# A graph-attention kernel on one core: the first turned block's copy, the order of SP's transfers, and row 5's high parts

## The chip, the cores and the metric

The kernel runs on one core of one Trainium2 chip. The time is the device time of one execution in microseconds, and the number compared is the median of several executions. The engines of the core are TensorE (PE in the profile), VectorE (DVE), ScalarE (ACT), GpSimd (POOL) and the sync engine (SP). Each works through its own instructions in order and waits on semaphores where another engine or a DMA has to be ready first. In this kernel nearly all DMAs are issued by SP.

## What is computed

```
Wh   = x @ W0.T                                # x: 4096 x 256
sim  = Wh @ Wh.T / (|Wh_i| |Wh_j| + 1e-8)
mask = (adj > 0) | eye                         # adj: 4096 x 4096
x1   = layernorm(x + softmax(where(mask, sim, -inf)) @ Wh)

m    = (adj > 0)
agg  = m @ x1 / max(rowsum(m), 1)
comb = [x1 @ W_self + b_self, agg @ W_nb + b_nb] @ W_comb + b_comb
out  = layernorm(x1 + relu(comb))
```

The similarity is symmetric, so the exponential of a block of scores serves twice: for the target rows it was made for, and turned (transposed) for the other side. The mask is not symmetric, so each of the two uses has its own block of `adj`.

## The kernel before

The 4096 nodes are 32 blocks of 128, in G = 8 groups of four blocks. The work is a triangle of group pairs, taken row by row: row `a` has its diagonal step (a, a) and then the pairs (a, b) with b > a. Row 0 uses an older scheme that the change does not touch. Rows 1 to 6 use the scheme called "far", with 6 + 5 + 4 + 3 + 2 + 1 = 21 pairs. Row 7 has only a diagonal. Behind the triangle come the value products and the second layer, which are almost only TensorE work.

One far pair (a, b) has eight tiles. Four are direct: TensorE multiplies the exponentials of blocks b*4 + r with the adjacency as columns of row a. In this text they are D0 to D3 (`attend_direct`). Four are turned: the same exponentials, transposed by DMA, give group b's partial sums. They are B0 to B3 (`attend_block`), one block of group b each. Every tile is 12 matmuls. TensorE's order within a pair is D0, D1, D2, D3, then S0' B0, S1' B1, S2' B2, S3' B3, where S0' to S3' are the next pair's scores (six matmuls each). In the last pair of a row (b = 7) the scores between are those of the next row's diagonal: none ahead of B0, one set ahead of each of B1, B2 and B3. The one ahead of B3 also waits until VectorE has masked the first diagonal tile (`prob_ready`).

The blocks B0 to B3 accumulate in two PSUM slots, `turned_ps(x % 2)`. So B2 writes where B0 was, and it waits (`turned_copied`, in `attend_block`) until VectorE has added B0's result into group b's partial sums in `big`. That addition is `block_copied` (L1079); for blocks 0 to 3 of the pair this text calls it C0 to C3. B3 waits for C1 in the same way, and the next pair's B0 and B1 for C2 and C3.

VectorE does for each pair, all in `pair_far`:

- K0 to K3 (`keep`, L1086): turns an adjacency unit of 128 x 1024 int32 into a float16 mask. It waits for the unit's load, `adj_loaded`.
- L0 to L3 (`low`, L1119): the low parts of the exponentials. Each waits for ScalarE's high part (L729), which follows ScalarE's exponential (L678), which follows the scores.
- M0 to M3 (`masked_parts`, L1091 and L1092): mask times high and mask times low, for the direct tiles.
- X0 to X3 (the same lines): the same for the turned tiles. X0 and X1 wait for part 0 of the transposes, X2 and X3 for part 1 (`far_loaded`).
- pieces of the previous row's residual and normalisation (`norm_work`), one list per row, handed out by `beside` and, for the first three, by the diagonal step.

Its order in a pair is K0 L0 C0 M0, L1 C1 M1, K1 L2 C2 M2, L3 C3 M3, K2 K3, X0 X1 X2 X3, where the C's belong to the pair before. So C0 of a pair stands behind X3, and behind the next pair's K0 and L0. In the last pair of a row C0 stands behind X3, the remaining pieces and `attention_out` (L1004), at the start of the next row's diagonal.

SP's order for a pair is in its own `pair_far`: wait for K0, load unit 0 of the next pair, wait for L1, issue the two transposes of part 0 (`turn_far`, L489), store unit 0's mask; wait for K1, load unit 1, store mask 1, wait for L3, issue the two transposes of part 1; load and store units 2 and 3. A load is 512 KB, a mask store 128 KB.

ScalarE makes exponentials, high parts and the byte masks (`unit_kept`, L713). The high half of a row's normalised features, `x1_hi`, is made by VectorE for rows 0 to 5 (`split_x1`, L1034) and by ScalarE for rows 6 and 7 (`x1_head`).

## Time and profile before

| | |
|---|---|
| median of 3 runs | 867.37 us (867.26 to 870.83) |
| the profiled execution, whole | 864.09 us |
| its span, first to last instruction | 862.3 us |
| mean granted TensorE clock | 0.996 |
| PE busy | 836.2 us, 97% |
| DVE busy | 589.6 us, 68% |
| ACT busy | 354.6 us, 41% |
| DMA, mean over the span | 172 GB/s; in the far rows 220 to 250 GB/s |

The far rows run from about 189 us to 580 us, row 7's diagonal ends at 590 us, and from there to the end TensorE computes with no wait but in the last few microseconds. Busy shares are means over the whole span; what bounds a stage has to be read from the waits in it. VectorE's recorded durations overlap a little (0.42 us recorded where the next instruction starts 0.34 us later), so a sum of durations is an upper bound of the time they take.

### The profile page before, as it was taken

What the parts mean: (1) busy time and instruction counts of PE and PEld (TensorE: products, weight loads), DVE (VectorE), ACT (ScalarE), POOL (GpSimd) and SP (SyncE); (2) the same over time, 40 slices, a digit from 0 to 9 for tenths busy, and PEclk for the clock granted to TensorE, in tenths of its full rate; (3) what the DMA queues carried; (4) which work ended last, traced back from release to release, by engine and by line L of the source; (5) the groups of instructions that cost most, each with busy time, mean ns of one, the idle gap of its engine ahead of it and who ended that gap; (6) DMA issues with size and microseconds to landing.
All of it is one profiled execution on the core that took longest, in us unless ns stands there. A gap on an engine that the chain in (4) does not pass through costs nothing.

```text
span 862.3 us, 18015 instructions
## 1 busy us (share of the span) xinstructions
PE 836.2 (97%) x6703; PEld 668.7 (78%) x6703; DVE 589.6 (68%) x1420; ACT 354.6 (41%) x577; POOL 74.0 (9%) x177
## 2 busy tenths in 40 slices
PE   8999999999999999999999999989999999999997
PEld 6867777777767677777777677768888888888886
DVE  2777887888688787888887989888445333333333
ACT  4867666665555555646546546445110000000000
POOL 2400000000000000000001101111101011100111
PEclk9999999999999999999999999999999999999999
DMA  8955666479999899999999999985303312330300
GB/s 211 242 153 171 163 175 174 126 203 225 229 220 232 241 225 233 236 253 226 239 259 223 233 246 230 247 181 220 51 8 128 117 51 85 111 114 22 116 20 19
DMA packets 202862, 147.93 MB, mean 172 GB/s; under 512 B 137505, under 2 KB 169778, under 8 KB 201746
## 3 DMA queue, kind: packets, MB, share of 16 engines
q1 hardware_dynamic: 202578, 146.33, 65.4%
q8 instruction: 53, 0.87, 0.4%
q0 software_dynamic: 192, 0.41, 0.2%
q14 instruction: 39, 0.32, 0.2%
HBM read 95.83 MB, written 20.99 MB: 135 GB/s over the span
## 4 chain that ended last, share of the span: by engine, by line
issue 80%; PE 10%; POOL 6%; DVE 2%; ACT 1%; POOLq 1%; DMA 0%; DVEq 0%; SPq 0%; ACTq 0%
POOL rstd L619 4%; PE ps L1294 4%; POOL var_eps L617 2%; PE ps L1384 1%; PE ps L1386 1%; PE ps L1385 1%; PE ps L1324 1%; PE ps L1326 1%; PE ps L1325 1%; ACT mask L690 1%; PE ps L1378 1%; DMA feat<-xT 0%; ACT prob_hi L685 0%; DVE feat L829 0%; DVE work L974 0%
## 5 line engine op out<-in xcount | busy, mean ns | idle before, releaser
L1384 PE MATMUL ps<-feat,prob_hi 128*128 128x257 f16 x1024 | 280.7, 274 | 14.5 <-DVE big L1079 12.5
L1386 PE MATMUL ps<-feat,prob_lo 128*128 128x257 f16 x1024 | 279.9, 273 | 0.0
L1385 PE MATMUL ps<-feat,prob_hi 128*128 128x256 f16 x1024 | 278.9, 272 | 0.0
L1554 PE MATMUL ps<-big,mgroup 128*128 128x257 f16 x992 | 219.2, 273 | 0.0
L1555 PE MATMUL ps<-big,mgroup 128*128 128x256 f16 x992 | 219.2, 273 | 0.0
L1384 PEld LDWEIGHTS ps<-feat,prob_hi 128*128 128x128 f16 x1024 | 99.9, 98 | 43.8 <-issue 18.7
L678 ACT ACTIVATE work<-ps 128x512 f32<-128x512 f32 (+2 forms) x144 | 79.9, 557 | 119.1 <-PE ps L1326 115.5
L1385 PEld LDWEIGHTS ps<-feat,prob_hi 128*128 128x128 f16 x1024 | 100.6, 98 | 24.4
L713 ACT ACTIVATE mask<-work 128x1024 fp8e4<-128x1024 f16 x84 | 86.2, 1050 | 76.6 <-DVE work L1086 76.6
L1386 PEld LDWEIGHTS ps<-feat,prob_lo 128*128 128x128 f16 x1024 | 99.7, 97 | 13.7
L1554 PEld LDWEIGHTS ps<-big,mgroup 128*128 128x128 fp8e4 x992 | 97.1, 98 | 12.1
L1555 PEld LDWEIGHTS ps<-big,mgroup 128*128 128x128 fp8e4 x992 | 97.1, 98 | 11.2
L1324 PE MATMUL ps<-unitT_lo,unitT_hi 128*128 128x512 f16 (+3 forms) x288 | 103.9, 362 | 1.0 <-DVE work L974 0.8
L1325 PE MATMUL ps<-unitT_hi 128*128 128x512 f16 (+3 forms) x288 | 103.8, 362 | 0.0
L1326 PE MATMUL ps<-unitT_hi,unitT_lo 128*128 128x512 f16 (+3 forms) x288 | 103.8, 362 | 0.0
L1091 DVE TENSOR_TENSOR prob_hi<-work,mgroup 128x512 f16<-128x512 f16 x168 | 70.5, 419 | 41.3 <-DMA mgroup<-mgroup 38.1
L981 DVE SCALAR_TENSOR_TENSOR prob_lo<-work,prob_hi 128x512 f16<-128x512 f32 x88 | 60.4, 687 | 22.6 <-ACT prob_hi L685 20.9
L1246 DVE TENSOR_SCALAR deg<-ps,ones,mix_scales 128x1 f32<-128x1 f32 x32 | 8.8, 275 | 94.7 <-PE ps L1555 94.7
L617 POOL TENSOR_TENSOR var_eps<-meanvar,ln_eps 128x1 f32<-128x1 f32 x64 | 16.6, 259 | 662.4 <-DVE meanvar L1021 441.5
L1092 DVE TENSOR_TENSOR prob_lo<-work,mgroup 128x512 f16<-128x512 f16 x168 | 70.1, 417 | 0.0
L1119 DVE SCALAR_TENSOR_TENSOR mgroup<-work,mgroup 128x512 f16<-128x512 f32 x84 | 57.7, 687 | 16.3 <-ACT mgroup L729 16.0
L685 ACT ACTIVATE prob_hi<-work 128x512 f16<-128x512 f32 x88 | 53.5, 625 | 33.9 <-DVE work L964 13.1
(130 smaller groups left out, 959.1 us busy)
## 6 DMA issues: line engine op xcount, KB each, us to landing
adj_sb<-adjT SPq DMA_DIRECT2D x128, 512.0 KB, 4.6
mask_spill<-mask SPq DMA_DIRECT2D x128, 128.0 KB, 4.1
mgroup<-mask_spill SPq DMA_DIRECT2D x8, 2048.0 KB, 8.3
xres<-x SPq DMA_DIRECT2D x8, 512.0 KB, 5.4
out<-rows SPq DMA_DIRECT2D x32, 128.0 KB, 1.7
feat<-xT SPq DMA_DIRECT2D x7, 512.0 KB, 7.1
norm_bc<-norm_row_dram SPq DMA_DIRECT2D x7, 256.0 KB, 4.1
mgroup<-mgroup SPq DMA_TRANSPOSE x84, 4.1
```

The costliest lines, as they stand in the source:

```text
L678: act.activation(expo[:, r, first:], score_ps(r)[:, first:], ACT.Exp, scale=1.0 / (UNIT_SCALE * UNIT_SCALE)).then_inc(exp_ready, 1)
L713: act.activation(mask[:, u % 4, :], kept(m), ACT.Copy, saturate=False).then_inc(mask_ready, 1)
L1091: dve.tensor_tensor(shaped(prob_hi[:, s, :]), adj, high, ALU.mult).then_inc(prob_ready, 1)
L1092: dve.tensor_tensor(shaped(prob_lo[:, s, :]), adj, low, ALU.mult).then_inc(prob_lo_ready, 1)
L1324: pe.matmul(to, unitT_hi[:, jb, k], unitT_lo[:, tgt, k], start=(k == 0), stop=False)
L1325: pe.matmul(to, unitT_hi[:, jb, k], unitT_hi[:, tgt, k], start=False, stop=False)
L1326: ins = pe.matmul(to, unitT_lo[:, jb, k], unitT_hi[:, tgt, k], start=False, stop=(k == KD - 1))
L1384: pe.matmul(acc(D + 1), prob_hi[:, s, cols], feat_hi_of(g)[:, r, 0:D + 1], start=start, stop=False)
L1385: pe.matmul(acc(D), prob_hi[:, s, cols], feat_lo_of(g)[:, r, :], start=False, stop=False)
L1386: return pe.matmul(acc(D + 1), prob_lo[:, s, cols], feat_hi_of(g)[:, r, 0:D + 1], start=False, stop=stop)
L1554: pe.matmul(agg_ps(q, D + 1), lhsT, z_hi_of(g)[:, r, 0:D + 1], start=(jb == 0), stop=False)
L1555: ins = pe.matmul(agg_ps(q, D), lhsT, z_lo_of(g)[:, r, :], start=False, stop=(jb == NB - 1))
```

## The change

Three things move, and nothing is computed otherwise.

1. VectorE makes C0 inside the turned part of its own pair: behind X1 and ahead of X2. Where the row goes on, the next pair's K0 and L0 go there too, ahead of C0.
2. SP issues the part-0 transposes ahead of load 0, and the part-1 transposes ahead of load 1.
3. ScalarE makes `x1_hi` of row 5. VectorE's four L1034 of that row are gone, and its low parts come one block later in the list of pieces.

```diff
+ACT_X1 = G - 3
@@ SP, pair_far
                 for m in range(4):
                     slot = (u0 + m) % 4
+                    if m < 2:
+                        turn_far(a, b, m)
                     sync.wait_ge(kept_ready, 4 * k + m + 1)
...
-                    if m == 0:
-                        turn_far(a, b, 0)
...
-                    if m == 1:
-                        turn_far(a, b, 1)
@@ ScalarE, pair_far
+                early_x1 = a - 1 == ACT_X1
+                if early_x1:
+                    x1_head(a - 1, 0)
                 unit_kept(u0 + 2, 2, 4 * k + 3)
+                if early_x1:
+                    x1_head(a - 1, 1)
                 unit_kept(u0 + 3, 3, 4 * k + 4)
+                if early_x1:
+                    x1_head(a - 1, 2)
+                    x1_head(a - 1, 3)
@@ VectorE, split_x1 and norm_work
-                if a < G - 2:
+                if a < ACT_X1:
...
-                lag = 1 if a < G - 2 else 2
+                lag = 1 if a < ACT_X1 else 2
@@ VectorE, diagonal
-                        block_copied(G - 1, j, t0 - GB + j)
-                        if j == 0:
+                        if j:
+                            block_copied(G - 1, j, t0 - GB + j)
+                        else:
                             dve.wait_ge(prob_lo_ready, t0)
@@ VectorE, pair_far
                 for r in range(GB):
+                    if r == 2:
+                        keep_unit(a, b, 1)
+                    if r or n == 0:
+                        if r == 0:
+                            keep_unit(a, b, 0)
+                        low_part(a, b, r)
+                        if n:
+                            block_copied(b - 1, r, t0 - GB + r)
...
                 for x in range(GB):
+                    if x == 2:
+                        if b < G - 1:
+                            keep_unit(a, b + 1, 0)
+                            low_part(a, b + 1, 0)
+                        block_copied(b, 0, t0 + GB)
```

VectorE between pair (2, 6) and pair (2, 7), before: X2 and X3 (the first four rows), a piece of normalisation, then the next pair's K0, L0, the copy C0 and M0. The "..." stands for the branch around a correction that is never taken here.

```order
L1091 TENSOR_TENSOR prob_hi<-work,mgroup 128x512
L1092 TENSOR_TENSOR prob_lo<-work,mgroup 128x512
L1091 TENSOR_TENSOR prob_hi<-work,mgroup 128x512
L1092 TENSOR_TENSOR prob_lo<-work,mgroup 128x512
L1028 TENSOR_SCALAR feat<-summed,meanvar,rstd 128x256
L1086 TENSOR_SCALAR work<-adj_sb 128x1024
...
L1119 SCALAR_TENSOR_TENSOR mgroup<-work,mgroup 128x512
L1079 TENSOR_TENSOR big<-big,ps 128x257
L1091 TENSOR_TENSOR prob_hi<-work,mgroup 128x512
L1092 TENSOR_TENSOR prob_lo<-work,mgroup 128x512
```

The same place in the changed kernel, from the end of X1 on (lines have shifted: L1094 is K, L1118 is L, L1087 is C, L1099 and L1100 are M and X, L1035 is the piece).

```order
L1094 TENSOR_SCALAR work<-adj_sb 128x1024
...
L1118 SCALAR_TENSOR_TENSOR mgroup<-work,mgroup 128x512
L1087 TENSOR_TENSOR big<-big,ps 128x257
L1099 TENSOR_TENSOR prob_hi<-work,mgroup 128x512
L1100 TENSOR_TENSOR prob_lo<-work,mgroup 128x512
L1099 TENSOR_TENSOR prob_hi<-work,mgroup 128x512
L1100 TENSOR_TENSOR prob_lo<-work,mgroup 128x512
L1035 TENSOR_SCALAR feat<-summed,meanvar,rstd 128x256
L1099 TENSOR_TENSOR prob_hi<-work,mgroup 128x512
L1100 TENSOR_TENSOR prob_lo<-work,mgroup 128x512
```

K0, L0 and C0 have moved from behind X3 and the piece to ahead of X2; M0 now follows the piece directly.

SP in one pair of row 2, before: load 0, part 0, store 0, load 1, store 1, part 1, load 2.

```order
L389 DMA adj_sb<-adjT 128x2x512
L489 DMA_TRANSPOSE mgroup<-mgroup 128x8x128 x2
L412 DMA mask_spill<-mask 128x1024
L389 DMA adj_sb<-adjT 128x2x512
L412 DMA mask_spill<-mask 128x1024
L489 DMA_TRANSPOSE mgroup<-mgroup 128x8x128 x2
L389 DMA adj_sb<-adjT 128x2x512
```

The same pair in the changed kernel.

```order
L490 DMA_TRANSPOSE mgroup<-mgroup 128x8x128 x2
L390 DMA adj_sb<-adjT 128x2x512
L413 DMA mask_spill<-mask 128x1024
L490 DMA_TRANSPOSE mgroup<-mgroup 128x8x128 x2
L390 DMA adj_sb<-adjT 128x2x512
L413 DMA mask_spill<-mask 128x1024
L390 DMA adj_sb<-adjT 128x2x512
```

Load 0 moved behind part 0, and load 1 with store 1 behind part 1.

ScalarE at the end of pair (6, 7) in the changed kernel, from the last high part (L733) to the next diagonal's first exponential (L677); before, the four rows L711 (`x1_head` of row 5) are not there and the masks L717 (L713 before) follow each other.

```order
L733 ACTIVATE mgroup<-work 128x512
L711 ACTIVATE big<-feat 128x256
L717 ACTIVATE mask<-work 128x1024
L711 ACTIVATE big<-feat 128x256
L717 ACTIVATE mask<-work 128x1024
L711 ACTIVATE big<-feat 128x256 x2
L669 COMPARE_AND_BRANCH
L669 UNCONDITIONAL_BRANCH
L677 ACTIVATE work<-ps 128x512
```

The last two of the four stand directly ahead of that exponential.

## Rows read from the trace of the kernel before

**Rows 1.** Waits view, PE: who it waited for, us in total, times, longest.

```profile
PE ps L1384 <- DVE big L1079: 12.5, 11, 2.5
PE ps L1384 <- DVE prob_lo L1092: 1.0, 1, 1.0
```

**Rows 2.** Timeline, PE: start us, us, instruction, idle before and releaser.

```profile
206.27 0.27 PE L1384 MATMUL ps<-feat,prob_hi 128*128 128x257 f16 x1 [1.60 <-DVE big L1079]
...
287.11 0.27 PE L1384 MATMUL ps<-feat,prob_hi 128*128 128x257 f16 x1 [1.41 <-DVE big L1079]
...
376.95 0.27 PE L1384 MATMUL ps<-feat,prob_hi 128*128 128x257 f16 x1 [1.19 <-DVE big L1079]
...
508.01 0.27 PE L1384 MATMUL ps<-feat,prob_hi 128*128 128x257 f16 x1 [1.70 <-DVE big L1079]
...
550.36 0.27 PE L1384 MATMUL ps<-feat,prob_hi 128*128 128x257 f16 x1 [1.50 <-DVE big L1079]
...
571.54 0.28 PE L1384 MATMUL ps<-feat,prob_hi 128*128 128x257 f16 x1 [1.01 <-DVE prob_lo L1092]
...
579.13 0.35 PE L1384 MATMUL ps<-feat,prob_hi 128*128 128x257 f16 x1 [2.50 <-DVE big L1079]
```

**Rows 3.** Windows: PE, PEld, DVE, ACT, POOL busy (count), PEclk, DMA share, GB/s.

```profile
400.00:450.00 50.00, 50.00 (x386) 37.45 (x385) 44.28 (x113) 26.52 (x37) 1.83 (x4) 1.00 0.97 252
576.70:579.10 2.40, 0.00 (x0) 0.00 (x1) 2.37 (x8) 0.46 (x1) 0.00 (x0) 1.00 0.23 45
579.13:582.65 3.52, 3.52 (x17) 2.56 (x18) 1.82 (x5) 0.63 (x1) 0.00 (x0) 0.52 1.09 214
```

**Rows 4.** Timeline, DVE, pair (2, 6): X2, then K0, L0 and C0.

```profile
357.51 0.42 DVE L1091 TENSOR_TENSOR prob_hi<-work,mgroup 128x512 f16<-128x512 f16 x1 [2.09 <-DMA mgroup<-mgroup]
...
359.52 0.69 DVE L1086 TENSOR_SCALAR work<-adj_sb 128x1024 f16<-128x1024 int32 x1
360.13 0.68 DVE L1119 SCALAR_TENSOR_TENSOR mgroup<-work,mgroup 128x512 f16<-128x512 f32 x1
360.73 0.41 DVE L1079 TENSOR_TENSOR big<-big,ps 128x257 f32<-128x257 f32 x1
```

**Rows 5.** Timeline, PE, the same pair: the first matmul of B0 and of B2.

```profile
356.24 0.27 PE L1384 MATMUL ps<-feat,prob_hi 128*128 128x257 f16 x1
...
361.48 0.27 PE L1384 MATMUL ps<-feat,prob_hi 128*128 128x257 f16 x1
```

**Rows 6.** Timeline, ACT, the same pair: the exponential and high part behind S0'.

```profile
356.44 0.60 ACT L678 ACTIVATE work<-ps 128x512 f32<-128x512 f32 x1 [1.36 <-PE ps L1326]
357.07 0.63 ACT L729 ACTIVATE mgroup<-work 128x512 f16<-128x512 f32 x1
```

**Rows 7.** Timeline, SP's issues, the same pair: load 0, part 0, load 1, part 1.

```profile
344.68 0.37 SPq L389 DMA_DIRECT2D adj_sb<-adjT  x1
346.93 2.60 SPq L489 DMA_TRANSPOSE mgroup<-mgroup  x2
...
350.20 1.17 SPq L389 DMA_DIRECT2D adj_sb<-adjT  x1
...
351.98 3.51 SPq L489 DMA_TRANSPOSE mgroup<-mgroup  x2
```

**Rows 8.** Waits view, DVE: its waits for the transposes.

```profile
DVE prob_hi L1091 <- DMA mgroup<-mgroup: 38.1, 19, 3.5
```

**Rows 9.** Source view of L389, the adjacency loads.

```profile
DMA to landing us min/median/max: 3.7/4.6/9.1
```

**Rows 10.** Source view of L489, the transposes.

```profile
DMA to landing us min/median/max: 3.1/4.1/6.3
```

**Rows 11.** Timeline, DVE, end of row 4: X2, C0, the next diagonal's first mask.

```profile
504.11 0.43 DVE L1091 TENSOR_TENSOR prob_hi<-work,mgroup 128x512 f16<-128x512 f16 x1 [2.15 <-DMA mgroup<-mgroup]
...
507.45 0.42 DVE L1079 TENSOR_TENSOR big<-big,ps 128x257 f32<-128x257 f32 x1
507.78 0.69 DVE L960 SCALAR_TENSOR_TENSOR work<-adj_sb,work 128x512 f32<-128x512 int32 x1
```

**Rows 12.** Lines view by form, DVE: the high parts of rows 0 to 5.

```profile
L1034 DVE TENSOR_SCALAR big<-feat 128x256 f16<-128x256 f32 x24 | 6.9, 286 | 0.1
```

More of the change, by code:

```diff
@@ L707, in diagonal, with x1_head @@
                         unit_mask(u % 4, j - 1, 16 * (u // 4))
+            def x1_head(a, q):
+                act.wait_ge(rows_ready, a * GB + q + 1)
+                act.activation(x1_hi_of(a)[:, q, :], x1_of(a)[:, q, :], ACT.Copy, scale=NORM_SCALE).then_inc(x1_hi_ready, 1)
             def unit_kept(u, m, count):
@@ L788, in value_heads @@
                                    ACT.Copy, scale=VALUE_SCALE).then_inc(z_hi_ready, 1)
-            def x1_head(a, q):
-                act.wait_ge(rows_ready, a * GB + q + 1)
-                act.activation(x1_hi_of(a)[:, q, :], x1_of(a)[:, q, :], ACT.Copy, scale=NORM_SCALE).then_inc(x1_hi_ready, 1)
             for q in range(2):
@@ L1032, in split_x1 @@
                 dve.wait_ge(rows_ready, a * GB + q + 1)
-                if a < G - 2:
+                if a < ACT_X1:
                     chain.join(chain.step(dve.tensor_scalar(x1_hi_of(a)[:, q, :], x1_of(a)[:, q, :], NORM_SCALE, None, ALU.mult)))
                 else:
-                    dve.wait_ge(x1_hi_ready, (a - G + 2) * GB + q + 1)
+                    dve.wait_ge(x1_hi_ready, (a - ACT_X1) * GB + q + 1)
                 dve.scalar_tensor_tensor(out=x1_lo_of(a)[:, q, :], in0=x1_of(a)[:, q, :], scalar=NORM_SCALE,
@@ L1092, in masked_parts, with keep_unit, low_part @@
                 dve.tensor_tensor(shaped(prob_lo[:, s, :]), adj, low, ALU.mult).then_inc(prob_lo_ready, 1)
+            def keep_unit(a, b, m):
+                n = b - a - 1
+                t0, _, u0 = (first + more for first, more in zip(tiles_before(a), (GB + n * STEP_TILES, 0, 2 + n * 4)))
+                if n:
+                    keep(u0 + m, m, t0 - STEP_TILES + 2 * (m + 1) if m < 2 else t0, u0 + m - 3)
+                else:
+                    keep(u0 + m, m, t0, u0 - 1 + m // 2)
+            def low_part(a, b, r):
+                n = b - a - 1
+                t0, f0, _ = (first + more for first, more in zip(tiles_before(a), (GB + n * STEP_TILES, GB + n * GB, 0)))
+                damping(a, b * GB + r, scores_before(a) + GB + n * GB + r, f0 + r, r)
+                dve.wait_ge(far_hi_ready, GB * (far_before(a) + n) + r + 1)
+                dve.wait_ge(prob_lo_ready, t0 - STEP_TILES + r + 1 if n else t0)
+                dve.scalar_tensor_tensor(out=far_parts[:, 1, r, :], in0=expo[:, r, :], scalar=PROB_SCALE, in1=far_parts[:, 0, r, :],
+                                         op0=ALU.mult, op1=ALU.subtract).then_inc(far_lo_ready, 1)
             def pair_far(a, b, between):
                 n = b - a - 1
-                t0, f0, u0 = (first + more for first, more in zip(tiles_before(a), (GB + n * STEP_TILES, GB + n * GB, 2 + n * 4)))
-                c0 = scores_before(a) + GB + n * GB
+                t0 = tiles_before(a)[0] + GB + n * STEP_TILES
                 k = far_before(a) + n
@@ L1106, in beside @@
                             between.pop(0)()
-                def keep_unit(m):
-                    if n:
-                        keep(u0 + m, m, t0 - STEP_TILES + 2 * (m + 1) if m < 2 else t0, u0 + m - 3)
-                    else:
-                        keep(u0 + m, m, t0, u0 - 1 + m // 2)
-                def low(r):
-                    dve.wait_ge(far_hi_ready, GB * k + r + 1)
-                    dve.wait_ge(prob_lo_ready, t0 - STEP_TILES + r + 1 if n else t0)
-                    dve.scalar_tensor_tensor(out=far_parts[:, 1, r, :], in0=expo[:, r, :], scalar=PROB_SCALE, in1=far_parts[:, 0, r, :],
-                                             op0=ALU.mult, op1=ALU.subtract).then_inc(far_lo_ready, 1)
-                for r in range(GB):
-                    if r % 2 == 0:
-                        keep_unit(r // 2)
-                    damping(a, b * GB + r, c0 + r, f0 + r, r)
-                    low(r)
-                    if n:
-                        block_copied(b - 1, r, t0 - GB + r)
+                for r in range(GB):
+                    if r == 2:
[4 more added lines that the diff above has]
+                        low_part(a, b, r)
+                        if n:
+                            block_copied(b - 1, r, t0 - GB + r)
                     dve.wait_ge(kept_ready, 4 * k + r // 2 + 1)
@@ L1132, in pair_far @@
                     beside()
-                keep_unit(2)
-                keep_unit(3)
+                keep_unit(a, b, 2)
+                keep_unit(a, b, 3)
                 beside()
```

## The prediction

> **What bounds the kernel now.** Four views, in this order. The page gives PE 97% busy, so the end is set by PE's work and the little idle time in it. The waits view for PE says what that idle time is: 12.5 us in 11 waits for VectorE's L1079, and 1.0 us in one wait for a turned tile [rows 1]. The timeline says where. L1079 is the copy of a finished block, and each of the 11 waits stands at the first matmul of a B2, whose PSUM slot B0 still holds. Four are at row ends, those of rows 1, 2, 4 and 5 (1.41, 1.19, 1.70 and 1.50, together 5.80 us). One is at the end of row 6 (2.50 us). Six are in the middle of rows: 1.60 us in the first pair of row 1, and five more that hold what is left, 12.5 - 5.80 - 2.50 - 1.60 = 2.6 us [rows 1, 2].
>
> The windows show something the waits view does not price. After the 2.50 us wait the granted clock is 0.52 for the next 3.52 us, that is the 1.2 GHz level, against 1.00 before and elsewhere [rows 3]. At half speed 3.5 us of work should have taken half as long, so this stretch lost about 1.7 us. No wait of 1.7 us or less is followed by it.
>
> VectorE is not the bound, but it is the engine that is late. In pair (2, 6) it waits 2.09 us at X2 for the part-1 transposes, and C0 comes behind X3, a piece, K0 and L0 [rows 4]. There B2 starts at 361.48, right behind its predecessor, and C0 ended at 361.14, with 0.3 us to spare [rows 4, 5]. That is how near every pair is to a wait. In all, VectorE waits 38.1 us for transposes, in 19 of the 21 pairs [rows 8].
>
> **Part 1: C0, with K0 and L0, ahead of X2.** No instruction is added. What matters is whether the new place adds a wait. I place the changed order in pair (2, 6). From B0 to B2 PE takes 5.24 us for four equal groups, 1.31 each, so B0 ends near 357.55 [rows 5]. C0 needs that, and L0 stands ahead of it. L0 needs ScalarE's high part, which ends at 357.70, since S0' ended only near 356.4 [rows 6]. L0 takes 0.60 us, so 358.3; C0 0.4, so 358.7; X2 is two instructions of 0.34, so 359.4. B2 wants both C0 and X2 by 361.4. So the new wait of VectorE (behind it are X2 and X3, and for X2 PE waits) takes the place of the wait for the transposes and leaves 2 us, where there were 0.3. The five small mid-row waits and the one of 1.60 should all go: **-4.2 us**. What comes next is C1 for B3. It follows X3, the piece, M0 and L1: 359.4 + 0.7 + 0.4 + 0.7 + 0.6, plus its own 0.4, gives 362.2, and B3 starts 2.6 us behind B2, at 364.1. Not late.
>
> At a row's end C0 stands alone ahead of X2, and there B0 is long finished when VectorE waits for the transposes, so C0 fits into that wait (2.15 us in row 4). What was behind it is then earlier by only 0.33 us. The next thing late is the first mask of the next diagonal: the scores ahead of B3 wait for it. In row 4 it ended near 508.4, so it would end near 508.1, while B2, starting 1.70 us earlier at 506.3 and 1.3 long, would end at 507.6 [rows 2, 11]. So about 0.5 us of row 4's 1.70 stays if X2 comes no sooner. The same working leaves 0.4 in row 5, 0.2 in row 1 and nothing in row 2, 1.1 together; earlier transposes (part 2) should return half of it. I take 0.6 kept of 5.80: **-5.2 us**.
>
> **Row 6.** Here VectorE has one pair for all the pieces and has no wait at X2, so C0's move alone shifts nothing behind it. B2 could start near 576.6 instead of 579.13 [rows 2]. The first mask ended near 579.5; with part 3 it ends near 578.4, against B2's end at 577.7. So about 0.8 of the 2.50 us stays: -1.7. A wait of 0.8 us is shorter than the many in this trace behind which the clock stays at 1.00 [rows 2], so the 1.7 us of half clock go as well. The 1.01 us wait for X0 [rows 2] shrinks by one high part less ahead of it, 0.29 us. Row 6 in all: 1.7 + 1.7 + 0.3 = **-3.7 us**.
>
> **Part 2: transposes ahead of loads.** No DMA is added. Part 0 moves past load 0, which waits for an early K0, so it gains little. Part 1 moves past load 1 and store 1. In pair (2, 6) it was issued 0.1 us behind store 1, and its first waits end at L3, so its issue gains 0.5 us at most; load 1, 512 KB issued 1.8 us ahead of it [rows 7], is no longer in its way. X2's data is then ahead of need. I book nothing for this beyond the 0.5 us at the row ends above.
>
> The price is on the loads. Load 0 was issued at 344.68 and would now be issued behind part 0, at 349.5 [rows 7], while K0 is wanted 4 us earlier than before. For K0 to hide it has to start at 357.1 (0.6 ahead of the high part's end), which gives the load 7.5 us; for B2 not to wait, at 359.2, which gives 9.6 us. Loads landed 3.7 to 9.1 us from issue, median 4.6 [rows 9]. Lower end 0, since the median is well inside; upper end 15 pairs (those with a next pair in their row) times the excess over 9.6. I take 0, nearest the median. Load 1 is issued near 355 instead of 350.2, and K1 comes near 363: covered.
>
> At this place the skill speaks against the change. The Trainium skill, "DMA: Bandwidth & Descriptors", section "Queues, rings and completion order", says that each DMA engine takes one queue's descriptors in ring order, so a load issued behind the transposes is read behind them. By that, and from rows: the second transpose is issued 1.3 us ahead of load 0 and lands after 4.1 (at most 6.3) [rows 7, 10], and then 4.6 us of load follow, so 7.4 us typically and 9.6 at worst, which just fits both limits. The sum stays as it is; the margin is thin, and this is the rival that ends slower.
>
> **Part 3: row 5's high parts on ScalarE.** Four instructions of 0.286 us leave VectorE [rows 12], 1.14 us, already booked in row 6. ScalarE gains four, and the last two stand ahead of the next diagonal's first exponential and wait for VectorE's pieces behind X1 and X2. That exponential would then end near 576.2, ahead of the mask that needs it (start 577.8). Cost 0; if VectorE's pieces came 2 us later it would cost that excess.
>
> **The sum.** 4.2 + 5.2 + 3.7 = 13.1 us. The profiled execution is 864.09 us whole, so it would be 851.0; the median of before is 867.37, 3.3 above it, and I apply the saving to the median: **854.3 us**. Behind 590 us PE has no wait until its last tile, and the pieces and transposes it needs there shift with row 7's end, so nothing is given back.
>
> **Rivals.**
> - *Row 6 keeps its wait and the half clock.* Its VectorE is the busiest (2.37 of 2.40 us ahead of the wait [rows 3]). If the new exponentials' order or the pieces hold the first mask, 1.7 + 1.7 us stay: 857.7. Chance 0.12.
> - *The wait moves on to the next late thing, C1 or the diagonal's first mask,* and half the gain is lost: 861. The slack found for C1 speaks against it, the row ends for it. Chance 0.11.
> - *DMA is the bound.* Its share is 0.97 [rows 3] and pairs follow each other no faster than their transfers: 867, or L0 ahead of C0 waits so long for ScalarE that C0 is no earlier, the change not doing what it says: also 867. But over 400 to 450 PE has no idle time at 252 GB/s, so the transfers can keep up. Chance 0.07 for both.
> - *Load 0 late: slower.* K0 stands ahead of X2 now, so a late load stops PE in 15 pairs. It decides from 9.6 us landing time on, breaks even at 9.6 + 13.1/15 = 10.5, and at 11.1 us costs 15 x 1.5 = 22.5: 867.4 - 13.1 + 22.5 = 876.8. The longest landing, 9.1 us, speaks against it. Chance 0.05.
> - *Everything goes,* the row ends' 0.6, row 6's 0.8 and the rest of X0's wait with it, 0.7: 852.2. Chance 0.05.
>
> **How the numbers follow.** The forecast of 854.3 has the chance left, 0.60. What a measurement of this kernel can tell from no change is about 0.5%, 4.3 us. Faster by more than that, below 863.0: 0.60 + 0.12 + 0.11 + 0.05 = 0.88. Within it: 0.07. Slower: 0.05. The range is from 851.3 (the best case and 0.9 for the spread of runs) to 861.5 (the third case); it leaves out 0.12, and some of the cases' own spread.
>
> **What the changed profile would show.** PE's waits for the copy line gone in mid-row, and at most 0.5 us in some row ends, now for the mask ahead of the diagonal scores. VectorE's 38 us wait for transposes mostly replaced by waits for ScalarE's high part at L0 and for PE at C0. The granted clock at 1.00 through the end of row 6. No wait of K for an adjacency load over 2 us. If VectorE waits on loads in most pairs and PE behind it, the fourth case holds and I am wrong; if PE's waits are gone and the time is still above 863, what I took as PE's own work was not.

## The result and the profile of the changed kernel

The changed kernel takes 855.62 us (median of 4, 855.06 to 857.24) against 867.54 us of the kernel before on the same chip (median of 4, 867.26 to 870.83). The ratio is 0.9857, with an interval of 0.983 to 0.9885. The forecast was 854.3, the range 851.3 to 861.5. So the sign and the size of the median are right. The profile shows that two steps under it were not.

The profiled execution of the changed kernel took 857.24 us whole (span 855.4), against 864.09 before. That is 6.9 us, where the sum said 13.1. First the waits of PE, as in [rows 1]: us in total, times, longest.

```profile
PE ps L1343 <- DVE work L971: 4.8, 4, 1.5
...
PE ps L1403 <- DVE prob_lo L1100: 2.2, 3, 1.6
...
PE ps L1343 <- DVE work L967: 0.5, 1, 0.5
```

The waits for the block copy, 12.5 us in [rows 1], are gone to the last one. What stands in their place is a wait of the scores (L1343) for VectorE's masks of the next diagonal (L971, and in row 6 L967), and a larger wait for X0 (L1100). L967 is the whole mask of a diagonal's first tile, and L967 and L971 together are the mask of a later one. The timeline of PE says where (start us, us, instruction, idle before and releaser); it is the counterpart of [rows 2].

```profile
289.50 0.39 PE L1343 MATMUL ps<-unitT_lo,unitT_hi 128*128 128x512 f16 x1 [1.24 <-DVE work L971]
...
451.22 0.39 PE L1343 MATMUL ps<-unitT_lo,unitT_hi 128*128 128x512 f16 x1 [1.19 <-DVE work L971]
...
508.73 0.39 PE L1343 MATMUL ps<-unitT_lo,unitT_hi 128*128 128x512 f16 x1 [0.87 <-DVE work L971]
...
539.34 0.28 PE L1403 MATMUL ps<-feat,prob_hi 128*128 128x257 f16 x1 [0.28 <-DVE prob_lo L1100]
...
551.70 0.39 PE L1343 MATMUL ps<-unitT_lo,unitT_hi 128*128 128x512 f16 x1 [1.51 <-DVE work L971]
...
565.29 0.28 PE L1403 MATMUL ps<-feat,prob_hi 128*128 128x257 f16 x1 [0.33 <-DVE prob_lo L1100]
568.36 0.28 PE L1403 MATMUL ps<-feat,prob_hi 128*128 128x257 f16 x1 [1.57 <-DVE prob_lo L1100]
...
575.35 0.28 PE L1343 MATMUL ps<-unitT_lo,unitT_hi 128*128 128x256 f16 x1 [0.47 <-DVE work L967]
```

No copy wait is left in mid-row. At the ends of rows 1, 3, 4 and 5 there are 1.24 + 1.19 + 0.87 + 1.51 = 4.81 us, where the row ends of before had 5.80 and row 3 had none. These four are not the wait for the diagonal's first mask that the prediction named. The waiting scores are 128x512, those of the next row's first pair, behind B3, and what they wait for is the mask of the diagonal's third tile. Only in row 6 do the scores ahead of B3 (128x256) wait for the first mask, 0.47 us. X0's wait there is 1.57, with 0.33 just ahead of it, and 0.28 is new in row 5.

VectorE's waits say what replaced the 38.1 us for transposes [rows 8].

```profile
DVE mgroup L1118 <- ACT mgroup L733: 36.1, 38, 2.5
...
DVE summed L1022 <- DMA xres<-x: 10.9, 6, 2.5
DVE big L1087 <- PE ps L1405: 5.8, 4, 1.8
...
DVE prob_hi L1099 <- DMA mgroup<-mgroup: 0.6, 1, 0.6
```

The low parts now wait for ScalarE's high parts, and the last copies for PE, as was foreseen. The line between them was not foreseen: 10.9 us of waiting for `xres`, the residual's rows of `x`, where before there was one wait of 0.7. L1022 is the first piece of the residual; it stands in the next row's diagonal behind the masks of the first two tiles, and the third tile's mask (L967 and L971) follows it. The five waits in rows 1 to 5 are 2.38, 1.27, 2.33, 1.83 and 2.48 us, and PE waits behind each but the 1.27 of row 2. In row 4, timelines of the changed kernel's SP and DVE:

```profile
500.70 0.43 SPq L548 DMA_DIRECT2D xres<-x  x1
```

```profile
507.19 0.48 DVE L1022 SCALAR_TENSOR_TENSOR summed<-summed,rsum_s,xres 128x256 f32<-128x256 f32 x1 [1.83 <-DMA xres<-x]
507.59 0.42 DVE L1087 TENSOR_TENSOR big<-big,ps 128x257 f32<-128x257 f32 x1
507.93 0.42 DVE L967 SCALAR_TENSOR_TENSOR work<-adj_sb,work 128x256 f32<-128x256 int32 x1
508.26 0.42 DVE L971 SCALAR_TENSOR_TENSOR work<-adj_sb,ps 128x256 f32<-128x256 int32 x1
```

And in the same row of the kernel before, where nothing waits:

```profile
504.32 0.48 SPq L549 DMA_DIRECT2D xres<-x  x1
```

```profile
510.52 0.48 DVE L1015 SCALAR_TENSOR_TENSOR summed<-summed,rsum_s,xres 128x256 f32<-128x256 f32 x1
```

VectorE wants the residual at 507.19 - 1.83 = 505.36 instead of 510.52, so 5.2 us sooner, and the load is issued only 3.6 us sooner. It also lands later after its issue. The source view gives us from issue to landing (minimum, median, maximum) of the kernel's eight loads of this kind; first before, then changed.

```profile
DMA to landing us min/median/max: 3.7/5.4/6.1
```

```profile
DMA to landing us min/median/max: 3.9/6.6/8.2
```

The middle of a row is as it was placed on paper. Pair (2, 6) in the changed kernel, DVE: L0, C0 and X2, the counterpart of [rows 4].

```profile
353.93 0.69 DVE L1118 SCALAR_TENSOR_TENSOR mgroup<-work,mgroup 128x512 f16<-128x512 f32 x1 [2.53 <-ACT mgroup L733]
354.53 0.42 DVE L1087 TENSOR_TENSOR big<-big,ps 128x257 f32<-128x257 f32 x1
354.87 0.42 DVE L1099 TENSOR_TENSOR prob_hi<-work,mgroup 128x512 f16<-128x512 f16 x1
```

B2 starts in that pair at 357.67 without a wait, 2.7 us behind C0's end, where before there were 0.3 us between them.

Last, the windows around row 6's wait (us, PE, PEld, DVE, ACT, POOL busy and count, granted clock, DMA share, GB/s), against [rows 3].

```profile
573.00:575.30 2.30, 1.87 (x16) 1.36 (x14) 2.30 (x8) 0.49 (x1) 0.00 (x0) 1.00 0.53 138
575.35:578.00 2.65, 2.65 (x27) 2.42 (x28) 2.45 (x7) 2.39 (x4) 0.00 (x0) 1.00 1.16 226
```

The clock stays at its 2.4 GHz level, where it had fallen to 0.52.

**The account.** From PE's last wait in row 0 to the first value product, before took 168.13 to 590.45, 422.3 us; changed, it takes 168.99 to 583.59, 414.6 us. "The stage" below is this stretch. It is 7.7 us shorter; the 0.86 us by which it starts later is ahead of anything the change touches and makes 6.9 of it. The terms that the rows of these two executions give: mid-row -4.2; row ends 4.81 against 5.80, -1.0; row 6's mask 0.47 against 2.50, -2.0; its half clock -1.7; X0 and its like 1.57 + 0.33 + 0.28 against 1.01, +1.2. The sum is -7.7.

### The profile page after: what moved, and what is told of

The parts are those of the page before. It is cut to its first block, busy times and chain, and to the rows that moved or that the text cites. A ratio compares the mean times of both kernels' runs of the same rounds, so it can differ in the third digit from the quotient of the medians.

```text
span 855.4 us, 18019 instructions
## 1 busy us (share of the span) xinstructions
PE 835.1 (98%) x6703; PEld 668.4 (78%) x6703; DVE 587.6 (69%) x1416; ACT 354.9 (41%) x581; POOL 71.6 (8%) x177
## 4 chain that ended last, share of the span: by engine, by line
issue 80%; PE 8%; POOL 6%; DVE 2%; ACT 2%; DMA 1%; POOLq 1%; SPq 0%; DVEq 0%; ACTq 0%
POOL rstd L618 4%; PE ps L1313 2%; POOL var_eps L616 2%; PE ps L1403 1%; PE ps L1405 1%; PE ps L1404 1%; DMA unitT_lo<-feat 1%; PE ps L1343 1%; PE ps L1345 1%; PE ps L1344 1%; PE ps L1397 1%; ACT mask L689 0%; SPq L434 0%; ACT rows L631 0%; ACT feat L643 0%
## 5 line engine op out<-in xcount | busy, mean ns | idle before, releaser
L677 ACT ACTIVATE work<-ps 128x512 f32<-128x512 f32 (+2 forms) x144 | 79.7, 555 | 109.0 <-PE ps L1345 105.5
L717 ACT ACTIVATE mask<-work 128x1024 fp8e4<-128x1024 f16 x84 | 86.2, 1049 | 68.4 <-DVE work L1094 68.4
L1343 PE MATMUL ps<-unitT_lo,unitT_hi 128*128 128x512 f16 (+3 forms) x288 | 103.7, 362 | 6.4 <-DVE work L971 4.8
L1405 PEld LDWEIGHTS ps<-feat,prob_lo 128*128 128x128 f16 x1024 | 99.5, 97 | 13.5
L1118 DVE SCALAR_TENSOR_TENSOR mgroup<-work,mgroup 128x512 f16<-128x512 f32 x84 | 57.9, 689 | 36.2 <-ACT mgroup L733 36.1
L1099 DVE TENSOR_TENSOR prob_hi<-work,mgroup 128x512 f16<-128x512 f16 x168 | 70.6, 420 | 3.4 <-DMA mgroup<-mgroup 0.6
L1100 DVE TENSOR_TENSOR prob_lo<-work,mgroup 128x512 f16<-128x512 f16 x168 | 70.3, 419 | 0.0
```

Source lines behind the costliest of these rows:

```text
L677: act.activation(expo[:, r, first:], score_ps(r)[:, first:], ACT.Exp, scale=1.0 / (UNIT_SCALE * UNIT_SCALE)).then_inc(exp_ready, 1)
L717: act.activation(mask[:, u % 4, :], kept(m), ACT.Copy, saturate=False).then_inc(mask_ready, 1)
L1099: dve.tensor_tensor(shaped(prob_hi[:, s, :]), adj, high, ALU.mult).then_inc(prob_ready, 1)
L1100: dve.tensor_tensor(shaped(prob_lo[:, s, :]), adj, low, ALU.mult).then_inc(prob_lo_ready, 1)
L1343: pe.matmul(to, unitT_hi[:, jb, k], unitT_lo[:, tgt, k], start=(k == 0), stop=False)
L1405: return pe.matmul(acc(D + 1), prob_lo[:, s, cols], feat_hi_of(g)[:, r, 0:D + 1], start=False, stop=stop)
```

## The experiments

Every experiment's ratio is to runs of the kernel before made with it, in one of three batches. Their medians are 865.99 us for the three parts apart, 867.40 for the changed kernel once more, the changed kernel without part 2, the residual loaded early and C0 alone, and 865.25 for K0 and L0 alone, both runs on row 6, and the early residual without part 2. The ratios are estimates from all the runs and differ a little from the quotient of the medians.

### The three parts apart

Part 1 alone: SP's order and row 5's high parts stay as they were before. Against the changed kernel:

```diff
-ACT_X1 = G - 3
+ACT_X1 = G - 2
@@ SP, pair_far
-                    if m < 2:
-                        turn_far(a, b, m)
...
+                    if m == 0:
+                        turn_far(a, b, 0)
...
+                    if m == 1:
+                        turn_far(a, b, 1)
```

> Only part 1 of the change: VectorE makes K0, L0 and C0 ahead of X2; SP's order and row 5's high parts are as before. Theory A (the place of C0 makes PE's waits, the transposes only fill VectorE's idle time): PE's 12.5 us of waits for the copy line go but for a rest at row ends, the time is 10 to 12 us below before, and VectorE still waits for the transposes at X2, some 10 to 20 us in all in place of 38. Theory B (the late part-1 transposes make C0 late, and the SP order is what counts): PE's waits move from the copy line to X2's lines, and the time is at most 5 us below before.

It takes 852.52 us, ratio 0.9847 (0.981 to 0.9885), with a stage of 411.7 us: part 1 alone is at least as fast as the whole change. The waits of PE and of DVE:

```profile
PE ps L1405 <- DVE prob_lo L1102: 2.4, 3, 1.8
PE ps L1345 <- DVE work L969: 2.1, 2, 1.6
```

```profile
DVE summed L1024 <- DMA xres<-x: 2.9, 3, 1.2
DVE prob_hi L1101 <- DMA mgroup<-mgroup: 2.7, 3, 1.3
```

The copy's line is gone and the row ends are clear but for 0.57 us in row 4, for the first mask, and 0.19 in row 5, for the third (the other 1.56 us are row 6's). VectorE waits 2.9 us for the residual, not 10.9. And it waits only 2.7 us for the transposes, in the old order of SP: most of the 38 us were time in which it had nothing else to do.

Part 2 alone: only SP's order, which is the first piece of the change's diff.

> Only part 2: SP issues the transposes ahead of loads 0 and 1; everything else is as before. Theory A: VectorE's wait at X2 shrinks from 38 us to 20 or less, C0 comes up to 1 us earlier, and since the five small mid-row waits are 0.3 to 0.7 us each and the four at row ends 1.2 to 1.7, some 4 to 6 us are gained; row 6 keeps its 2.5 us and its half clock. Theory B: nearly all of the change's 12 us are gained. Theory C (the loads pay for it): VectorE waits for adjacency loads at K and the time is above before.

859.31 us, 0.9925 (0.9901 to 0.9949), stage 417.9. DVE's waits:

```profile
DVE prob_hi L1089 <- DMA mgroup<-mgroup: 26.8, 17, 2.9
...
DVE summed L1013 <- DMA xres<-x: 9.0, 6, 2.3
```

By itself part 2 gains, since X2 is on the way to C0 there and VectorE waits 11 us less in sum for its transposes. The price is already in the second line: 9.0 us for the residual, and behind it 1.5 us of PE's waits for the third mask, in rows 1, 2 and 4.

Part 3 alone: only row 5's high parts, the change's pieces on ScalarE and in `split_x1` and `norm_work`.

> Only part 3: ScalarE makes row 5's high parts, as in the changed kernel. Expected by my working: row 6 alone moves, by 0.3 us at X0 and 0.9 to 1.1 us at C0, so 1.2 to 1.4 us, and up to 3 us if the wait that is left, 1.4 us, no longer brings the half clock behind it. Rival: ScalarE's waits for VectorE's pieces hold the next diagonal's first exponential, and the time is that of before or 1 us above.

862.69 us, 0.9961 (0.993 to 0.9993). The profiled execution's row 6, PE (X0, then B2):

```profile
574.21 0.28 PE L1393 MATMUL ps<-feat,prob_hi 128*128 128x257 f16 x1 [0.78 <-DVE prob_lo L1101]
...
580.79 0.27 PE L1393 MATMUL ps<-feat,prob_hi 128*128 128x257 f16 x1 [1.49 <-DVE big L1088]
```

Against [rows 2] the wait for X0 falls from 1.01 to 0.78 and B2's from 2.50 to 1.49, so 1.2 us, about the 1.14 that four instructions took from VectorE. The median is 3.3 us below that of the runs beside it, more than these two waits, but the interval reaches from 0.6 to 6 us; what the rest is was not shown.

The kernel before, once more:

> The kernel before, unchanged, for a second profile. Its first profiled execution took 864.09 us where its median was 867.4. If its waits vary from execution to execution (the transposes' landing times decide them), this profile shows more than 13.5 us of PE waits for VectorE in the far rows, some 16 to 17 us where it takes 867; if they do not vary, the 3.3 us lie elsewhere, in the first 60 us or the tail.

861.05 us in this one execution, stage 418.7 against 422.3 of the first profile. The copy's waits are 10.3 us in 10 instead of 12.5 in 11; at the row ends they are 3.46 instead of 5.80, in mid-row 4.33 and 4.21. And the clock stays at 1.00 behind row 6's wait: from its end to the first value product it is 9.66 us here and 11.32 in the first profile, for the same work. The two together, 2.2 and 1.7 us, are about the difference of 3.6. Executions of before differ by this much, which matters for the account below.

### Which part costs: the changed kernel without part 2, and a residual loaded early

The changed kernel, once more, in one batch with the next two and with C0 alone:

> The changed kernel once more, on the same chip as the three below, so that they can be compared with it. Theory A (from the first runs: part 2 holds back the residual's load at row ends, and gives nothing that part 1 has not given): ratio 0.985 to 0.987, VectorE waits about 11 us for the residual's load in 6 waits, and PE about 5 us in 4 or 5 waits for a diagonal's mask. Rival B (the 10.9 us of that wait were one execution's luck): this profile shows them at 3 us or less.

855.29 us, 0.9875 (0.9847 to 0.9904), with 10.0 us for the residual. The third mask's waits at the row ends come to 3.82 us, in all five rows. Set beside the 3.46 to 5.80 us of the two profiles of before, the row ends gained little or nothing by the change.

Parts 1 and 3, with SP's order of before (the diff of part 1 alone, with `ACT_X1 = G - 3` kept):

> Parts 1 and 3 without part 2: SP keeps the old order. Theory A: 2 to 4 us faster than the changed kernel, since the residual's load is issued and lands earlier; VectorE waits 3 us or less for it; 1 us or so faster than part 1 alone by row 6. Rival C (part 2 pays by its earlier transposes): equal to the changed kernel or slower, with VectorE waiting over 10 us for transposes.

850.76 us, 0.9828 (0.9799 to 0.9856), stage 409.2. This is 4.5 us less than the changed kernel beside it. DVE waits 2.0 us for the residual and 3.3 us for the transposes. So part 2 costs about 4.5 us once part 1 is there, and its own object, the transposes' wait, is worth 3 us of an engine that is not the bound. What part 2 did bring is the little that the prediction booked for it: without it PE waits in row 4 for the diagonal's first mask, where the prediction worked out 0.5 us, and with it this wait is nowhere.

```profile
500.37 0.28 PE L1345 MATMUL ps<-unitT_lo,unitT_hi 128*128 128x256 f16 x1 [0.60 <-DVE work L969]
```

The changed kernel, with the residual's load of rows 1 to 5 moved in SP's queue: in the row's last pair, right behind the part-1 transposes and so ahead of loads 1 to 3, instead of behind all of them.

```diff
@@ SP, pair_far
                     if m < 2:
                         turn_far(a, b, m)
+                    if m == 1 and b == G - 1 and a < G - 2:
+                        sync.wait_ge(summed_ready, a * GB)
+                        sync.dma_start(xres[:, :, :], x_v[a]).then_inc(xres_loaded, 16)
@@ SP, behind the row's pairs
-                wait(sync, summed_ready, a * GB)
-                sync.dma_start(xres[:, :, :], x_v[a]).then_inc(xres_loaded, 16)
+                if not FIRST_FAR <= a < G - 2:
+                    wait(sync, summed_ready, a * GB)
+                    sync.dma_start(xres[:, :, :], x_v[a]).then_inc(xres_loaded, 16)
```

> The changed kernel, with one more move: in the last pair of rows 1 to 5 SP issues the residual's load right behind the part-1 transposes, ahead of load 1, not behind the last store. Theory A: the waits for the residual's load go (from 11 us to 1 or less, row 0's), the waits of PE for a diagonal's mask shrink from 5 us to 1 or less, and the time is 3 to 4 us below the changed kernel. Rival D (PE's waits at row ends come from the diagonal's own chain, mirror and exponential): the VectorE waits go, PE's stay, and the time is that of the changed kernel within 1 us.

849.49 us, 0.9811 (0.9783 to 0.9839), stage 408.0: the fastest, 5.8 us under the changed kernel beside it. The waits of DVE and, from PE's timeline, all that is left of waits for VectorE between 200 and 600 us:

```profile
DVE summed L1026 <- DMA xres<-x: 0.9, 1, 0.9
```

```profile
533.37 0.28 PE L1407 MATMUL ps<-feat,prob_hi 128*128 128x257 f16 x1 [0.25 <-DVE prob_lo L1104]
...
559.81 0.28 PE L1407 MATMUL ps<-feat,prob_hi 128*128 128x257 f16 x1 [1.19 <-DVE prob_lo L1104]
...
566.80 0.28 PE L1347 MATMUL ps<-unitT_lo,unitT_hi 128*128 128x256 f16 x1 [0.47 <-DVE work L971]
```

The masks' waits at the ends of rows 1, 3, 4 and 5 are all gone with the residual's. That the residual's load held PE through the third tile's mask is thus shown, not only read from the order.

The same without part 2 (parts 1 and 3, SP's old order; the residual's load again right behind the part-1 transposes, which there is behind load 1 and store 1):

> Parts 1 and 3 with the old order of SP, but the residual's load of rows 1 to 5 issued behind the part-1 transposes of the row's last pair. Theory A (part 2 gives nothing once part 1 is there): as fast as the changed kernel with the early residual's load, 0.980 to 0.982 of before, within 1 us of it. Rival: 1 to 2 us slower than that one, with VectorE waiting 3 us or more for transposes.

851.08 us, 0.9847 (0.9818 to 0.9876), stage 409.2. In this batch the kernel with all three parts, the early residual and a small change in row 6 (the last experiment below, which gains nothing by that change) takes 849.58. So with the residual out of its way part 2 is worth about 1.5 us, where with it in the way it cost 4.5. In the profiled executions the stages are 409.2 and 408.4 us and PE's waits in them 2.1 and 2.0; where the 1.5 us come from stays open.

### What part 1 consists of

Part 1 moves two things, C0 and the next pair's K0 and L0. C0 alone (K0 and L0 stay at the pair's start), against part 1 alone:

```diff
@@ VectorE, pair_far
-                    if r or n == 0:
-                        if r == 0:
-                            keep_unit(a, b, 0)
-                        low_part(a, b, r)
-                        if n:
-                            block_copied(b - 1, r, t0 - GB + r)
+                    if r == 0:
+                        keep_unit(a, b, 0)
+                    low_part(a, b, r)
+                    if n and r:
+                        block_copied(b - 1, r, t0 - GB + r)
...
                     if x == 2:
-                        if b < G - 1:
-                            keep_unit(a, b + 1, 0)
-                            low_part(a, b + 1, 0)
                         block_copied(b, 0, t0 + GB)
```

> Of the change only the copy C0 moved ahead of X2; K0 and L0 stay behind X3, and SP and row 5's high parts are as before. Theory A (PE waited for C0 and for nothing else): as fast as part 1 as a whole, 0.984 to 0.987 of before. Rival E (K0 and L0 have to use VectorE's idle time, or C1 and M0 become late by their 1.2 us): PE waits for M0 or for C1 in mid-row, some 0.5 us in a third of the 15 pairs, and the time is 2 to 3 us above part 1 alone.

864.60 us, 0.9981 (0.9961 to 1.0001), stage 423.3: hardly anything. PE's waits and DVE's wait for PE:

```profile
PE ps L1401 <- DVE prob_lo L1102: 5.3, 7, 1.8
PE ps L1341 <- DVE work L969: 4.4, 5, 1.7
...
PE ps L1401 <- DVE big L1089: 2.9, 7, 1.2
```

```profile
DVE big L1089 <- PE ps L1403: 24.6, 19, 2.4
```

C0 now stands where B0 is not finished yet, and VectorE waits 24.6 us for PE with nothing else ahead. X2 and X3 then come late, and so do K0 and L0 behind them, and PE waits mostly for masked turned tiles and the diagonal's first mask instead of for the copy. The theory that the copy's new place is what counts falls.

K0 and L0 alone, with C0 where it was, behind X3:

```diff
@@ VectorE, pair_far, against the kernel before
                 for r in range(GB):
-                    if r % 2 == 0:
-                        keep_unit(r // 2)
...
-                    low(r)
+                    if r == 2:
+                        keep_unit(a, b, 1)
+                    if r or n == 0:
+                        if r == 0:
+                            keep_unit(a, b, 0)
+                        low_part(a, b, r)
...
                 for x in range(GB):
+                    if x == 2 and b < G - 1:
+                        keep_unit(a, b + 1, 0)
+                        low_part(a, b + 1, 0)
```

> The other half of part 1: K0 and L0 ahead of X2, C0 stays behind X3 and the pieces (at row ends where it was). SP and row 5's high parts as before. Theory F (VectorE has no time to wait for PE at C0 unless the next pair's K0 and L0 are out of the way; what counts is that 1.2 us of work go into its idle time): C0 comes 0.5 to 1.2 us earlier than before, the six mid-row waits go (4.2 us in the first profile), the five at row ends and row 6 stay, and the time is 4 to 7 us below before. Theory G (only C0 ahead of X2 helps, together with K0 and L0): no mid-row wait goes, and the time is that of before within 2 us.

858.10 us, 0.9924 (0.9896 to 0.9951), stage 416.5. PE, first mid-row wait and row 4's end:

```profile
203.97 0.27 PE L1402 MATMUL ps<-feat,prob_hi 128*128 128x257 f16 x1 [0.15 <-DVE big L1088]
...
501.74 0.27 PE L1402 MATMUL ps<-feat,prob_hi 128*128 128x257 f16 x1 [1.58 <-DVE big L1088]
```

The six mid-row waits have shrunk to this one of 0.15 us, though the copy has not passed X2 and X3: 1.3 us of work had left the stretch ahead of it and filled the idle time behind X1, and VectorE's wait for transposes fell from 38 to 10.0 us. The row ends (4.1 us in all, 1.58 of it in row 4, where it was 1.70) and row 6's 2.50 stay, since there is no next pair's K0 and L0 there. So in the middle of rows it is the work moved into the idle time that pays, and C0's own move pays at row ends, where X2's wait is the idle time: about 7 us for the first alone, 2 us (within its uncertainty) for the second alone, 13.5 us for both.

### Row 6

The kernel before, with C0 moved in row 6 only:

```diff
@@ VectorE, diagonal
-                        block_copied(G - 1, j, t0 - GB + j)
+                        if j or a < G - 1:
+                            block_copied(G - 1, j, t0 - GB + j)
@@ VectorE, pair_far
                 for x in range(GB):
+                    if x == 2 and a == G - 2:
+                        block_copied(b, 0, t0 + GB)
```

> The kernel before, with the copy C0 ahead of X2 in row 6's single pair alone. Of PE's waits only the longest, 2.50 us, changes: by my working 1.1 us of it stay. Theory H (a long wait lowers PE's clock only in some executions, and the clock is a large part of how executions of one kernel differ): 1.5 to 3.5 us below before in the median, the mean granted clock of its executions 0.001 or so above before's. Rival: no clock effect, 1.2 to 1.5 us below and the same mean clock.

864.40 us, 0.9999 (0.9971 to 1.0026). PE waits 1.57 us for the first mask where it waited 2.50 for the copy:

```profile
578.43 0.28 PE L1327 MATMUL ps<-unitT_lo,unitT_hi 128*128 128x256 f16 x1 [1.57 <-DVE work L960]
```

The wait falls by 0.9 us, as the trace has it, and the median by 0.85 us, which is within the uncertainty. The 2 to 3 us that a half clock gone as well would have brought are not seen, though the interval, which reaches to 2.5 us, does not quite exclude them.

Row 6 is VectorE's. In the version with the early residual the pieces of normalisation in row 6 were put off, so that X0 comes sooner (places by which so many pieces are done):

```diff
+ROW6_PIECES = (0, 1, 2, 3, 4, 5, 7, 9, 12, 14)
@@ VectorE, pair_far, beside
-                    for _ in range(place * share // (STEP_TILES + 1) - (place - 1) * share // (STEP_TILES + 1)):
+                    done = ROW6_PIECES if a == G - 2 else [p * share // (STEP_TILES + 1) for p in range(STEP_TILES + 2)]
+                    for _ in range(done[place] - done[place - 1]):
```

> The changed kernel with the early residual's load, and in row 6 two of the pieces of normalisation handed out behind X0 and not ahead of it. Theory J (in row 6 VectorE's own chain sets X0, so what PE gained before comes to a wait there): PE's wait of 1.2 us at X0 goes to 0.3 or less; the pieces come later, so the wait for the diagonal's first mask, 0.5 us, grows by 0 to 0.5; 0.5 to 1.2 us faster than without. Rival K (row 6 as a whole is VectorE-bound, the work only moves): the wait at X0 goes, the one for the mask grows by as much, and the time is equal within 0.4 us.

849.58 us, 0.9829 (0.98 to 0.9858), stage 408.4: no gain. PE in row 6:

```profile
559.93 0.28 PE L1409 MATMUL ps<-feat,prob_hi 128*128 128x257 f16 x1 [0.68 <-DVE prob_lo L1105]
...
567.56 0.28 PE L1349 MATMUL ps<-unitT_lo,unitT_hi 128*128 128x256 f16 x1 [1.11 <-DVE work L972]
```

1.19 + 0.47 has become 0.68 + 1.11. VectorE's work in row 6 sets the end of the row, and this order only moves the place where PE waits for it.

## Why the prediction came out as it did

**What bounds the kernel.** Right. PE's idle time in the far rows was the whole of what could be had, and with nearly all of it gone the stage is at 408 us.

**Part 1, mid-row, -4.2.** Right in size and in its working: the wait at L0 for ScalarE's high part took the place of the wait for the transposes, and C1 was not the next thing late. The text did not ask which of the moved instructions earned it. The run of K0 and L0 alone shows that they did; C0's own move was needed at row ends.

**The row ends, -5.2 with 0.6 left.** Wrong: 4.81 us stayed. The first mask, the next late thing that the text named, was rightly sized for row 4: 0.5 us foreseen, 0.57 and 0.60 in the two kernels without part 2. (Of the 0.4 of row 5 the trace of before gives only 0.2 to 0.3, and no wait for it came there.) The step "earlier transposes (part 2) should return half of it" held too, and more than half. What failed is the step before it, that behind this mask nothing else would be late. In the changed kernel all 4.81 us are waits for the third tile's mask, which stands on VectorE behind the residual's first piece, and that piece waits for a load that part 2 had made late.

**Part 2, nothing but the 0.5.** Wrong: it costs 4.5 us. The text priced load 0 and load 1 for the K's that want them and stopped there. In row 4 the transposes stood between load 1 and the rest before; now load 1 stands behind them, and SP's issues go straight from it to loads 2 and 3 and the residual's load. First before, then changed:

```profile
496.21 0.44 SPq L389 DMA_DIRECT2D adj_sb<-adjT  x1
```

```profile
497.19 0.58 SPq L390 DMA_DIRECT2D adj_sb<-adjT  x1
```

So the residual's load comes 3.5 us behind load 1's issue, where it came 8.1 us behind it. On it the normalisation's first piece and, in order behind it, the third mask depend. It was wanted 5.2 us sooner in row 4, issued 3.6 us sooner, and took longer from issue to landing, at the median 6.6 us instead of 5.4. The rule cited from the Trainium skill ("DMA: Bandwidth & Descriptors", "Queues, rings and completion order") was the right one to weigh, and it was applied to the wrong load. The trace is in line with it: 4.7 us at the median from issue to landing for the five residual loads issued ahead of loads 1 to 3, against 6.6 for the changed kernel's eight, most of them behind such loads.

**Load 0 late, the slower rival.** It did not happen: no K waits for a load. In the working's own pair K0 starts without a wait 5.8 us behind load 0's issue. From issue to landing the loads take 4.8 us at the median (before 4.6). The longest landing rose to 10.1 us from 9.1, in the source view of all loads; it held up no K.

```profile
DMA to landing us min/median/max: 3.7/4.8/10.1
```

**Row 6, -3.7.** The mask's wait (0.8 foreseen, 0.47 measured) and the clock (1.00) are as foreseen. The -0.3 at X0 is wrong: PE waits 1.2 us more there and at the two places like it. The text took X0's lateness as fixed and PE's arrival too. But PE, having lost its other waits, is ready for X0 3.7 us sooner than before, and VectorE has it only 3.2 us sooner. The run with the pieces put off did not buy this off inside row 6.

**Part 3.** Right in mechanism: alone it takes 1.2 us off row 6's two waits.

**Why the median still fits.** The sum for one profiled execution was 13.1 and the pair of profiles shows 6.9; the errors at the row ends (4.2) and at X0 (1.5) account for most of the difference, and 0.9 is the start of the stage. The medians differ by 11.9 us, since the profiled execution of before was one of its faster ones and the one of after the slowest of four: in the 58 executions of before made beside the experiments the time went from 860.37 to 871.68 with a median of 865.7, and 15 of them were below the profiled 864.09. So that the median was met to 1.3 us is in part luck. The sum was 6.2 us too large for the rows that it was worked out from, and nearly as much came back from elsewhere: the median of before lies 3.5 us above its profiled execution, and that of the changed kernel 1.6 us below its own. What those 3.5 us are, the last section says as far as it is known.

## What to carry to other kernels

Work moved into an engine's idle time pays by what it takes off the path behind it; ask of each moved instruction whether it is the one that pays, and test it alone. When a queue's order is changed, price every transfer to the end of the queue's stretch, the small ones for the next stage above all, and against the time at which a now faster engine will want them. If a wait shrinks where the late engine is the bound of its stage, look for the same time at that engine's next consumer.

## What the hardware showed beyond that

**The same wait does not always lower the clock.** In [rows 3] the clock was 0.52 behind a wait of 2.50 us, and the text took that as a rule. Windows of four other executions, at the same kind of place (columns as in [rows 3]): part 2 alone and K0 and L0 alone, both behind 2.50 us in row 6; the kernel before once more, behind 2.50 us in row 6; part 3 alone, behind 3.18 us at the end of row 1.

```profile
574.12:577.60 3.48, 3.48 (x19) 2.60 (x20) 2.12 (x6) 0.63 (x1) 0.00 (x0) 0.56 1.06 226
```

```profile
572.40:576.00 3.60, 3.60 (x23) 2.81 (x24) 2.48 (x6) 1.04 (x3) 0.00 (x0) 0.66 1.04 209
```

```profile
577.75:581.25 3.50, 3.50 (x32) 3.13 (x33) 2.81 (x7) 1.84 (x4) 0.00 (x0) 1.00 1.04 220
```

```profile
291.23:294.70 3.47, 3.47 (x32) 3.10 (x33) 3.40 (x10) 1.81 (x4) 0.00 (x0) 1.00 0.90 201
```

The price is best read from the end of row 6's wait to the first value product, which is the same work in all. It takes 11.32 us in the first profile of before, 11.32 in part 2 alone and 11.33 in K0 and L0 alone, and 9.66 in the kernel before once more and in part 3 alone, where the clock stayed at 1.00. So each low stretch cost 1.66 us, as the prediction had it from the clock alone (1.7). In K0 and L0 alone it begins later, and the window above holds only part of it. A wait like these is thus a risk, not a certainty. The Trainium skill ("TensorE: Matmul & The Clock Gate", Part 1, on the clock gate) ties the lower level to idle time of the engine; the three low stretches are in line with it, and the other two show that a wait's length alone does not decide.

**The clock goes with the spread of the times.** Over the 58 executions of before, time and mean granted clock have a correlation of -0.74. The 20 with a clock of 0.998 or more took 863.4 us in the mean, the 28 from 0.995 to 0.997 took 866.2, and the 10 of 0.994 or less took 868.2. The changed kernel and all that hold both halves of part 1 stayed at 0.998 to 1.000, and their own runs spread over 1.4 to 2.4 us, where those of before spread over 6 to 10 in each batch. It is a correlation, and removing the row 6 wait in part (1.57 us left) left the mean clock at 0.997 as it was in the kernel before beside it. The profiles allow an estimate of the clock's share. In the far rows of all fourteen the clock falls only in the three stretches priced above; these three executions have a mean clock of 0.996 or 0.997, the others of 0.999 or 1.000. So one such stretch is about 0.003 of the mean clock and 1.66 us. By that the fastest and the slowest group, 0.005 apart, differ by some 2 to 3 us of the measured 4.8 through the clock, the rest being longer waits; and of the 11.9 us between the medians of the first comparison about 1.7 would be the clock's. It is an estimate: no run takes the clock apart from the waits ahead of it.
